# Gated attention's output projection and linear layer as three-pass products, with the low halves' places in the queues

## What is computed

```python
out = jax.nn.silu(g) * o @ Wout            # o: attended rows, centred, divided by their deviation per head
x1 = x0 + out
xn = layernorm(x1)                         # rows of 512
q, scales = mx_quantize(xn)                # blocks of 32, fp6 grid
x2 = x1 + (q * scales) @ weight + bias     # L0_ffn_weight, 512 x 512
xn4 = layernorm(x2)                        # input of layer 1's cross attention
k = ctx @ Wk + bk ; v = ctx @ Wv + bv ; query = xn4 @ Wq + bq
```

## Time and profile before

| | us |
|---|---|
| median of 3 runs | 1193.2 |
| lowest, highest | 1188.41, 1195.52 |
| the profiled execution | 1191.81 |
| its span, first to last instruction | 1190.5 |
| mean granted TensorE clock, share of full | 0.996 |

### The profile page before, as it was taken

How to read it: one execution, slowest core, us unless ns; L and a number is a source line. 1 busy time by engine, 2 the same in 40 slices (tenths; PEclk the granted TensorE clock), 3 DMA queues, 4 the chain that set the end, 5 groups by cost and what they waited for, 6 DMA issues and landing times.

```text
span 1190.5 us, 21697 instructions
## 1 busy us (share of the span) xinstructions
PE 1143.4 (96%) x8729; PEld 848.7 (71%) x8729; DVE 744.6 (63%) x1505; ACT 536.0 (45%) x1032; POOL 236.7 (20%) x292
## 2 busy tenths in 40 slices
PE   7999999989989999999999999999999999999997
PEld 5654477766547677777777777777787668887886
DVE  6457387678685665565566666665895767455632
ACT  3334346853212655555565656555553332223421
POOL 2300013066550061121212122211531100000000
PEclk9999999999999999999999999999999999999999
DMA  9759700110305155454444444454800402224211
GB/s 349 271 212 393 285 13 1 36 45 1 107 18 176 21 105 125 93 100 92 92 89 90 90 89 96 92 101 74 117 6 1 79 1 36 36 36 65 42 36 35
DMA packets 325671, 111.57 MB, mean 94 GB/s; under 512 B 301834, under 2 KB 302908, under 8 KB 321348
## 3 DMA queue, kind: packets, MB, share of 16 engines
q1 hardware_dynamic: 324224, 109.11, 36.5%
q10 hardware_dynamic: 1348, 1.09, 0.3%
HBM read 65.59 MB, written 20.97 MB: 73 GB/s over the span
## 4 chain that ended last, share of the span: by engine, by line
PE 84%; DVE 8%; ACT 4%; POOL 1%; issue 1%; DMA 1%; POOLq 0%; SPq 0%; DVEq 0%; ACTq 0%
PE bank L292 59%; PE bank L1845 3%; PE bank L1861 2%; PE bank L571 2%; PE bank L589 2%; PE bank L1152 2%; PE bank L1131 2%; PE bank L248 2%; DVE W L1394 1%; PE bank L507 1%; PE bank L238 1%; PE bank L1100 1%; PE bank L1084 1%; PE bank L1108 1%; PE bank L2268 1%
## 5 line engine op out<-in xcount | busy, mean ns | idle before, releaser
L1791 POOL COPY PT<-W 32x512 f32<-32x512 f32 x120 | 84.3, 703 | 311.3 <-DVE W L1984 246.3
L1973 DVE CUSTOM_DVE_ANT_0 W<-bank,W 128x512 f32<-128x512 f32 x128 | 80.8, 688 | 102.4 <-PE bank L1845 100.7
L2049 ACT ACTIVATE K<-bank,vecT 128x512 f32<-128x512 f32 x64 | 43.8, 690 | 166.9 <-PE bank L292 166.9
L2070 ACT ACTIVATE W<-W,low 128x512 f32<-128x512 f32 x128 | 90.7, 711 | 25.9 <-DVE low L1973 25.9
L292 PE MATMUL bank<-xT,wT 128*128 128x512 f32 x384 | 92.5, 390 | 0.8 <-ACT W L2933 0.5
L292 PE MATMUL bank<-Wkv,Wq 128*128 128x512 f32 x384 | 92.4, 395 | 0.0
L292 PE MATMUL bank<-Wkv,ctxT 128*128 128x512 f32 x384 | 91.8, 395 | 0.0
L292 PE MATMUL bank<-Wq,Wkv 128*128 128x512 f32 x384 | 89.9, 390 | 1.6 <-DVE Wq L309 1.6
L292 PE MATMUL bank<-ctxT,Wkv 128*128 128x512 f32 x384 | 89.8, 392 | 0.0
L292 PE MATMUL bank<-woT,hR 128*128 128x512 f32 x384 | 87.8, 390 | 0.7 <-DVE W_late L2854 0.5
L292 PEld LDWEIGHTS bank<-Wkv,ctxT 128*128 128x128 f32 x384 | 70.8, 188 | 22.2 <-ACT K L2049 5.7
(11 more groups left out here) (352 smaller groups left out, 2106.4 us busy)
## 6 DMA issues: line engine op xcount, KB each, us to landing
PT<-W SPq DMA_DIRECT2D x360, 64.0 KB, 2.1
W<-ctx_turned SPq DMA_DIRECT2D x16, 1024.0 KB, 5.7
W<-in_ctx_dram SPq DMA_DIRECT2D x8, 1024.0 KB, 10.1
ctx_turned<-ctxT SPq DMA_DIRECT2D x8, 1024.0 KB, 7.7
ctx_turned<-W SPq DMA_DIRECT2D x8, 1024.0 KB, 6.9
XT<-in_ctx_dram SPq DMA_DIRECT2D x4, 1024.0 KB, 12.0
XT<-in_L_ffn_wi_dram SPq DMA_DIRECT2D x64, 64.0 KB, 2.1
raw_own<-in_ctx_dram SPq DMA_DIRECT2D x3, 1024.0 KB, 11.2
```

What stands on the lines that cost most here:

```text
L1791: pool.tensor_copy(there, here).then_inc(kept_p.s, 1)
L1973: dve.tensor_tensor_reduce(out=PR[:, j, :], in0=bank[:, 4 + j % 4, :], in1=mask, scale=1.0, scalar=3.0e38, op0=ALU.add, op1=ALU.min, accum ...
L2049: act.activation(K[:, m, :], bank[:, n % 4, :], ACT.Identity, bias=pcol("L1_xattn_bk", m)).then_inc(ring_a.s, 1)
L2070: act.activation(PR[:, j, :], PR[:, j, :], ACT.Exp, bias=low[:, j:j + 1], scale=-1.0, accum_out=total[:, j:j + 1]).then_inc(expd.s, 1)
```

## The change

Both products take the three-pass form. For the output projection ACT makes y's high half (`y_high_a`, after `normal_v`), and POOL its low half (`y_low_pool`), and `project_pe` waits for that. For the linear layer ACT writes the high half of the turned blocks (`blocks_a`, as a rounding copy, one buffer instead of two) and DVE the low half (`rows_low_v`), behind `quantise_v`. The weights' halves are made once, Wout's on ACT ahead of pass 1 and on DVE in pass 1, the linear weight's on ACT in pass 1 and on POOL in passes 1 and 2. The key weights' halves move to passes 2 to 4. On PE `variance_pe` stands ahead of `project_pe`. Layer 1's rows are normalised by ACT instead of DVE, for which DVE negates the mean and POOL multiplies it by rstd (`shift`). The low halves of Wq move from DVE to POOL. Wq's high half now waits for the last output product, its low half for the last linear product.

```diff
+        def normalise_a(xn, g):
+            act.wait_ge(rstd_ok.s, rstd_ok(nth("rstd", 3, g)))
+            act.activation(xn[:, g, :], X[:, g, :], ACT.Identity, scale=rstd[:, g:g + 1],
+                           bias=shift[:, g:g + 1]).then_inc(kept["normed_a"].s, 1)
...
+            if negated:
+                v(dve.tensor_scalar(shift[:, g:g + 1], mv[:, g, 0:1], -1.0, None, ALU.mult))
...
+            if l == 3:
+                p(ins)
+                ins = pool.tensor_tensor(shift[:, g:g + 1], shift[:, g:g + 1], rstd[:, g:g + 1], ALU.mult)
...
+            key_chunks = {2: (0, 1), 3: (2,), 4: (3,)}
...
                     if t <= G:
                         deviation_pool(t - 1)
+                    if t <= 2:
+                        for c in (2 * t - 2, 2 * t - 1):
+                            linear_weight_pool(c)
+                    if 3 <= t < G + 3:
+                        row_stats_pool(2, t - 3)
                     if 4 <= t < G + 4:
                         bias_pool(t - 4)
-                    if 3 <= t < G + 3:
-                        row_stats_pool(2, t - 3)
+                    if 2 <= t < G + 2:
+                        y_low_pool(t - 2)
+                for c in range(C):
+                    query_weight_pool(c)
...
+            def y_low_pool(g):
+                pool.wait_ge(high_w.s, high_w(g))
+                split_pool(y_low[:, g % 3, :], y[:, g % 3, :], y_high).then_inc(low_w.s, 1)
...
             def project_pe(g):
-                pe.wait_ge(ynm.s, ynm(g))
+                if g == 0:
+                    pe.wait_ge(wt_v.s, wt_v(15))
+                pe.wait_ge(low_w.s, low_w(C + g))
...
-                for c in range(C):
-                    ins = pe.matmul(bank[:, 7, :], y[:, g % 3, c * P:(c + 1) * P], slot(7)[:, c, :], start=(c == 0), stop=(c == C - 1))
-                ins.then_inc(proj.s, 1)
+                halves_of_y = (y_high, y_low[:, g % 3, :])
+                product(bank[:, 7, :], lambda h, c: halves_of_y[h][:, c * P:(c + 1) * P], lambda h, c: Wout[h][:, c, :],
+                        C).then_inc(proj.s, 1)
...
             def linear_pe(g):
-                pe.wait_ge(xt_a.s, xt_a(G + g))
+                pe.wait_ge(xt_v.s, xt_v(g))
...
-                for c in range(C):
-                    ins = pe.matmul(bank[:, linear_at(g), :], xd[:, g % 2, c * P:(c + 1) * P], slot(8)[:, c, :], start=(c == 0), stop=(c == C - 1))
-                ins.then_inc(proj.s, 1)
+                product(bank[:, linear_at(g), :], lambda h, c: xd[:, h, c * P:(c + 1) * P], lambda h, c: Wlin[h][:, c, :],
+                        C).then_inc(proj.s, 1)
...
+                    if 1 <= t <= G:
+                        variance_pe(t - 1)
                     if 3 <= t < G + 3:
                         project_pe(t - 3)
-                    if 1 <= t <= G:
-                        variance_pe(t - 1)
...
+            def rows_low_v(g):
+                dve.wait_ge(xt_a.s, xt_a(G + g))
+                split_v(xd[:, 1, :], bank[:, 6, :], xd[:, 0, :]).then_inc(xt_v.s, 1)
...
                     if 4 <= t < G + 4:
                         quantise_v(t - 4)
+                    if 5 <= t < G + 5:
+                        rows_low_v(t - 5)
...
-                    if G + 4 <= t:
-                        for c in range(2):
-                            query_weights_v(2 * (t - G - 4) + c)
-                    if 7 <= t:
-                        normalise(xn4, 3, t - 7)
...
             def blocks_a(g):
                 act.wait_ge(turned.s, turned(2 * G + g))
-                if g >= 2:
-                    act.wait_ge(proj.s, proj(linear[g - 2]))
-                act.copy(xd[:, g % 2, :], bank[:, 6, :]).then_inc(xt_a.s, 1)
+                if g:
+                    act.wait_ge(proj.s, proj(linear[g - 1]))
+                split_a(xd[:, 0, :], bank[:, 6, :]).then_inc(xt_a.s, 1)
+
+            def y_high_a(g):
+                act.wait_ge(ynm.s, ynm(g))
+                if g:
+                    act.wait_ge(proj.s, proj(out[g - 1]))
+                split_a(y_high, y[:, g % 3, :]).then_inc(high_w.s, 1)
...
                 gate_out_a(7)
-                for t in range(1, G + 5):
+                for c in range(C):
+                    out_weights_a(c)
+                for t in range(1, G + 6):
                     if t <= G:
                         attended_a(t - 1)
                     if t + 1 < G:
                         sigmoid_a(t + 1)
+                    if 3 <= t < G + 3:
+                        y_high_a(t - 3)
...
+                    if 7 <= t:
+                        normalise_a(xn4, t - 7)
```

More of the change, by code:

```diff
@@ L114, in map_of_stages_4_and_5 @@
             first.close()
+            keep(first, "WL", "W_low", [P, 2, C, D], F32R)
+            first.close()
             keep(at, "bq", "bq5", [P, D])
@@ L123, in map_of_stages_4_and_5 @@
             keep(at, "Wo", "half_x", [P, 2, C, 512], F32R)
-            keep(second, "Wq", "Wq4", [P, 2, C, D], F32R)
+            keep(second, "ctxT_even", "ctxT_even", [P, 2, C, NK], F32R)
             keep(first, "half_x1", "half_x1", [P, 2, C, 512], F32R)
@@ L908, in l0_gated_attention @@
             xb_high = sb(late, "xb_high", [P, C, ROWS], F32R)
-            y = W[:, 0, 0:3, :]
+            y, y_low, y_high = W[:, 0, 0:3, :], YX[:, 0, 0:3, :], YX[:, 0, 3, :]
             amax = sb(ph, "amax", [P, G, D // 32])
             inv = sb(ph, "inv", [P, D // 32])
-            xd, scratch, row = W[:, 1, 0:2, :], W[:, 1, 2, :], W[:, 1, 3, :]
-            Wkv, ctxT, raw = kept["Wkv"], kept["ctxT"], slot(4)
+            xd, scratch, row = YX[:, 1, 0:2, :], W[:, 1, 2, :], W[:, 1, 3, :]
+            Wkv, ctxT, raw, Wq = kept["Wkv"], kept["ctxT_even"], slot(4), kept["ctxT_odd"]
+            normed_a = kept["normed_a"]
+            Wout = (kept["ctxT_odd"][:, 0, :, :], kept["WL"][:, 0, :, :])
+            Wlin = (kept["ctxT_odd"][:, 1, :, :], kept["WL"][:, 1, :, :])
             raw_in, ring, ctx_a, ctx_v = (kept[name] for name in ("raw_in", "ring", "ctx_a", "ctx_v"))
@@ L957, in l0_gated_attention @@
                         made[g] = G + 24 + len(out) + len(linear)
+            for l in (4, 5):
+                for g in range(G):
+                    side_by_side["normed", l, g] = (l - 1) * G + g
             summed = lambda l, g: xsum(nth("xsum", l, g))
@@ L1349, in stats_of_v, with out_weights_v @@
                 dve.wait_ge(xsum.s, summed(l, g))
-                row_stats_v(g)
+                row_stats_v(g, negated=(l == 2))
+            def rows_low_v(g):
+                dve.wait_ge(xt_a.s, xt_a(G + g))
+                split_v(xd[:, 1, :], bank[:, 6, :], xd[:, 0, :]).then_inc(xt_v.s, 1)
+            def out_weights_v(c):
+                dve.wait_ge(wt_a.s, wt_a(12 + c))
+                split_v(Wout[1][:, c, :], slot(7)[:, c, :], Wout[0][:, c, :]).then_inc(wt_v.s, 1)
             def quantise_v(g):
@@ L1480, in vector @@
                         stats_of_v(2, t - 6)
-                    if 1 <= t <= C:
-                        key_weights_v(t - 1)
+                    if t == 1:
+                        for c in range(C):
+                            out_weights_v(c)
+                    for c in key_chunks.get(t, ()):
+                        key_weights_v(c)
                     if t == G + 3:
@@ L1562, in blocks_a, with out_weights_a, linear_weights_a @@
                 act.wait_ge(turned.s, turned(2 * G + g))
-                if g >= 2:
-                    act.wait_ge(proj.s, proj(linear[g - 2]))
-                act.copy(xd[:, g % 2, :], bank[:, 6, :]).then_inc(xt_a.s, 1)
+                if g:
[6 more added lines that the diff above has]
+                split_a(y_high, y[:, g % 3, :]).then_inc(high_w.s, 1)
+            def out_weights_a(c):
+                act.wait_ge(slot_in[7].s, slot_in[7]())
+                split_a(Wout[0][:, c, :], slot(7)[:, c, :]).then_inc(wt_a.s, 1)
+            def linear_weights_a(c):
+                split_a(Wlin[0][:, c, :], slot(8)[:, c, :]).then_inc(wt_a.s, 1)
             def key_weights_a(c):
@@ L1573, in query_weights_a @@
                 act.wait_ge(slot_in[2].s, slot_in[2]())
-                split_a(kept["Wq"][:, 0, c, :], W[:, 2, c, :]).then_inc(wt_a.s, 1)
+                if c == 0:
+                    act.wait_ge(proj.s, proj(out[G - 1]))
+                split_a(Wq[:, 0, c, :], W[:, 2, c, :]).then_inc(wt_a.s, 1)
             def context_a(c):
@@ L1653, in scalar @@
                         square_a(t - 1)
-                    if t >= 5:
+                    if 5 <= t < G + 5:
                         blocks_a(t - 5)
-                    if t <= C:
-                        key_weights_a(t - 1)
+                    if t == 1:
+                        for c in range(C):
+                            linear_weights_a(c)
+                    for c in key_chunks.get(t, ()):
+                        key_weights_a(c)
                     if t == G + 3:
@@ L1886, in tensor @@
                         pe.wait_ge(xt_a.s, xt_a.base)
```

(5 more changed lines are left out.)

60 lines of the change are left out of this document (36 added, 24 removed).

## The result

| | before | after |
|---|---|---|
| median, us | 1193.2; 1193.9 of 83 executions | 1204.34 |
| lowest, highest | 1188.19, 1198.68 | 1201.0, 1205.38 |
| profiled execution, its span | 1191.81, 1190.5 | 1201.0, 1199.7 |
| mean granted clock, profiled execution | 0.996 | 0.992 |
| mean granted clock, median of all executions | 0.994 | 0.987 |

The change makes the kernel slower: ratio 1.0088, 95% interval 1.0063 to 1.0113. The forecast was 1194.2 in 1187 to 1202, so it fell outside the range on the slow side.

A forecast was written before the change was run, and what follows sets the result against it. PE, busy 96% of the span, was taken as the bound. Cheaper products' gains in passes 6 to 8 were outweighed by losses in passes 3 to 5 and the tail: +0.7, plus 0.3, giving 1194.2 us, range 1187 to 1202.

The forecast's parts named there:

- the sum: All passes and the tail together: +0.7 us, plus 0.3 for more meetings of DVE and POOL; span 1191.5.
- Passes 9 and 10: Two more hand-offs of y eat the products' gain: 9.1 us each, -0.3 and +0.3.
- Products: Sixteen output and linear products on PE fall from 3.43 to about 2.8 us each, 10.6 us in all.
- Passes 1 and 2: Wout's four casts on ACT delay the attended copy, so the mean waits 0.3 to 0.4 us: +0.4.
- Passes 3 to 5: Variance loses its cover and waits for ACT's square, pass 3 also for POOL's low half: +2.7 us together.
- Passes 6 to 8: Linear product and turn cover the variance, so the gain arrives: -1.9, -1.9 and -1.3 us.
- The tail: Passes 11 to 13 to the first key product: DVE's order makes the linear products late, +2.7 on 13.13 us.
- Behind the tail: ACT's last normalisation and POOL's low halves of Wq, done at about 24 us before a query product at 32, cost nothing.
- Rival 1: Slower: POOL and DVE hold each other up at the splits and y's low half; 1202 us, chance 0.20.
- Rival 2: Faster: ACT's copy and square and POOL's low half come sooner, the gain arrives on PE; 1186 us, chance 0.16.
- Rival 3: Products dearer, from alternating weights and starting behind small instructions: sixteen lose 4.8 us; 1199 us, chance 0.06.

The follow-up runs named there:

- e1: The changed kernel with ACT's wait for POOL's memset of the carrier moved to the carrier's first use; 1201.93 us, ratio 1.0062.
- e2: The changed kernel with DVE's tail order altered: group 6's low half before quantising group 7, context's low halves after group 7's; 1200.3 us, ratio 1.0044.
- e4: The changed kernel with the linear weight's second pair of low halves on POOL moved from pass 2 to pass 3; 1202.45 us, ratio 1.0057.
- e5: The changed kernel with three orders altered together: DVE's tail, POOL's second pair of linear-weight low halves, ACT's carrier wait; 1196.46 us, ratio 1.0029.
- e3: The changed kernel with nine matmuls nobody reads in PE's waits of passes 1 to 3 and the tail; 1199.12 us, ratio 1.0031.
- e7: The change's linear-layer part alone against the kernel before; output projection stays full-precision, with the variance behind it; 1193.59 us, ratio 1.001.
- e6: The changed kernel with the variance's matmuls back behind the output product on PE; 1204.49 us over two executions, ratio 1.0104.

## Why the prediction was wrong

**What the clock cost, and what the order cost.** After against before, the medians differ by 10.4 us. At equal clock they differ by 4.6 (1199.9 and 1195.3); the rest, some 6 us, goes with 0.007 less clock, for which before's own slope would give 7.2. With that slope the order costs 3.6 and the clock nearly 7; the split is good to about 1 us. The filling gives the clock's part back by experiment: 5.2 us. So the step that failed is first of all one that the sum did not have. It took each product at 2.8 us, "at full flow", also behind waits of 1 to 4 us that the same text had worked out. The text named a falling clock in its last line as what would make it wrong, and gave it neither price nor chance. A price could have been estimated: one product at half the clock is 2.8 us more, with a wait of 4 us ahead of it in the tail and two waits ahead of it in pass 3 (in after's profile these two products cost 2.4 and 1.7 us more). Passes 9 and 10, where the text had PE waiting too, are the third place: the profiles of e1, e2, e4 and e5 all have falls there.

Of the order's 3.6 to 4.6 us the sum had 1.0. What it missed, by the parts below, is 0.5 in pass 3, 0.8 in passes 9 and 10 and 1.2 behind the tail; together with the 1.0 that is 3.5, and what is left is of the size of the error and stays open.

**Products.** The price at full clock nearly holds: 2.9 us in e3, and 0.68 less for each of passes 6 and 7 in e7. Behind a wait it is 3.04 to 3.08.

**Passes 1 and 2**, forecast +0.4: 6.67 and 6.46 against twice 6.46, +0.2. Nearly right.

**Passes 3 to 5.** Forecast 10.4, 9.7 and 9.7; measured 12.59, 9.77 and 9.87. The waits were the named ones in the named order. Pass 3 missed by 2.2: product 0 at the lower clock, 1.7, and a later start in the pass, 0.5, nearly all of it POOL's second power, which took 3.35 us where 2.9 was taken (the first, 3.29, was taken as 3.3). The walk's own terms give 10.2 for pass 3, not 10.4, which changes little.

**Passes 6 to 8.** Forecast 11.5, 11.5 and 10.7; measured 11.48, 11.48 and 10.75. Right, and by its own reason: e6 brings back 0.6 us when the variance goes back.

**Passes 9 and 10.** Forecast 9.1 each, measured 9.48 and 9.53 at full clock. The chain was right, as these rows of PE and POOL in pass 10 show; the hand-offs took 0.15 more and the product behind its wait 0.28 more than taken.

```profile
346.69 1.27 POOL L331 TENSOR_TENSOR YX<-W,YX 128x512 fp32r<-128x512 f32 x1 [1.41 <-ACT YX L318]
```

```profile
348.01 0.50 PE L310 MATMUL bank<-ctxT_odd,YX 128*128 128x512 f32 x1 [1.32 <-POOL YX L331]
```

**The tail.** Forecast 15.8, measured 17.45. The start of linear product 6 was right to 0.1 us; its length, 5.47 us, and with it the turn, the half and the low half of group 7 behind it, was not. With the clock held (e3) the same order took 15.06, so the walk was right, and long by 0.7. e2 took the wait from 4.15 to 1.40, and that order alone could have been had in advance from the order of DVE's instructions that stands above.

**Behind the tail.** "They cost nothing" was said of POOL's four low halves of Wq, since the query product comes late. That was right for the query product, which waits for DVE (1.75 us) and not for them, and false of what stands behind them in POOL's queue. The memset was among the rows, and who waits for it was not looked up. 1.1 us, by e1.

**The rivals.** Rival 1 gave nearly the right time for the wrong reason. POOL does hold DVE up: in pass 8 two of DVE's rows stretch from 0.54 and 0.43 us beside POOL's bias (325.57, 1.30 us) and gating (329.34, 1.30 us),

```profile
325.64 1.51 DVE L250 TENSOR_SCALAR XT<-X,mv,rstd 128x512 f32<-128x512 f32 x1 [0.33 <-POOL rstd L236]
...
329.37 1.55 DVE L292 TENSOR_SCALAR W<-XT 128x512 fp8e4<-128x512 f32 x1
```

and yet pass 8 kept its forecast to 0.05, since it had the slack; y's low half took 1.3 us on average and 1.47 at most, so it was hardly held up. Rival 2 is false: the waits came as walked. (Its 1186 is about 1 us more than its own terms give.) Rival 3 is false where the clock is full. What it describes, a product dearer than forecast, is true behind a wait, by 0.25 us, and not for the alternating weights. "That a falling clock makes the waits dear" should have been the fourth.

## What to carry to other kernels

On a kernel whose matrix engine is busy 96% of the span, every wait that a change adds has two prices: the wait, and the chance that the work behind it runs at half clock. Price both, and compare versions at equal granted clock as well as by time, or an accident of the profile is taken for the change. When a batch of work is put on a queue, list everything behind it on that queue up to the next barrier, small instructions too, and ask who waits for each: an 0.1 us memset cost 1.1 us here.

## What was not expected of the hardware

- The level fell after waits of 1.3 us in passes 9 and 10 in e1 (0.77 there) and e2 (0.76), and did not fall with the same waits after, though PE runs the same code in e1 and after up to there; it did not fall before, with a wait of 1.48 us. So one profile does not tell which waits are met. What decides it in one execution stays open.
- Nine matmuls of no use made the changed kernel 5.2 us faster, with 0.0075 more mean clock.
- Among 83 executions of one unchanged program, 0.001 of mean granted clock went with 1.03 us, over a range of 0.009: most of the 10 us between its lowest and highest time.
